# Matmuls of a constant ahead of TensorE's waits in the last batches of a graph-attention kernel's first stage

## The reference

```python
h = maximum(layernorm(x), 0)
Wh = (h @ W).reshape(N, 4, 32)                     # layer 0: attention, four heads
e = leaky_relu(s_src[:, None, :] + s_dst[None, :, :])
att = softmax(where(adj > 0, e, -9e15), axis=1)
x = x + elu(einsum('ijh,jhd->ihd', att, Wh))
h = maximum(layernorm(x), 0)
x = x + where(has_nbr, max over neighbours j of h[j], 0)    # layer 1: maximum
```

## Time and profile before

| | us |
|---|---|
| median of 3 runs | 626.85 (613.61 to 634.16) |
| the profiled execution | 619.35, span 617.6 |
| PE busy / DVE busy / POOL busy | 348.8 / 350.5 / 332.1 |
| ACT busy | 154.7 |
| stage one's part of the span | up to about 381.6 |
| mean granted TensorE clock | 0.715 of full |

### The profile page before, as it was taken

One profiled execution on the slowest core, in us unless ns is written; L12 is line 12 of the kernel. 1 busy time (PEld: TensorE's weight loads), 2 busy tenths in 40 slices (PEclk: granted clock), 3 DMA queues, 4 the chain that ended last, 5 costly groups with the idle time before them and its releaser, 6 DMA issues. The chain is left out here.

```text
span 617.6 us, 8203 instructions
## 1 busy us (share of the span) xinstructions
PE 348.8 (56%) x2410; PEld 258.7 (42%) x2410; DVE 350.5 (57%) x1375; ACT 154.7 (25%) x429; POOL 332.1 (54%) x360
## 2 busy tenths in 40 slices
PE   1847667592939385461707371511755666566764
PEld 1732334361617153251707370301643554455553
DVE  7976767772928284572818656311644554454575
ACT  1731312321314142432413242100111111121122
POOL 7927075254555637274563703774665666666620
PEclk9958588697878879595856696555677667666578
DMA  8938999994979869127120401121121122222211
GB/s 294 418 127 314 399 357 402 364 377 145 369 237 382 296 247 339 50 57 287 41 55 10 136 26 51 52 55 34 47 53 47 48 59 57 55 57 64 61 39 33
DMA packets 28740, 100.97 MB, mean 163 GB/s; under 512 B 6869, under 2 KB 13397, under 8 KB 20501
## 3 DMA queue, kind: packets, MB, share of 16 engines
q1 hardware_dynamic: 16245, 76.33, 31.8%
q0 software_dynamic: 9344, 19.75, 13.1%
q10 hardware_dynamic: 3104, 4.33, 1.9%
HBM read 93.92 MB, written 6.46 MB: 163 GB/s over the span
## 5 line engine op out<-in xcount | busy, mean ns | idle before, releaser
L711 POOL DMA_INDIRECT G<-wh_table,idx x146 | 149.3, 1022 | 112.2 <-DVE idx L1266 70.8
L1481 POOL DMA_INDIRECT G<-h_table,idx x146 | 137.8, 944 | 75.9 <-issue 35.5
L1546 DVE TENSOR_TENSOR_SCAN S<-adjf,S,psf 128x128 f32<-128x128 bf16 x107 | 51.0, 477 | 83.8 <-remote 38.7
L1513 PE MATMUL psf<-identf,S 128*128 128x128 f32 x146 | 58.1, 398 | 71.5 <-issue 53.7
L1522 PE MATMUL psf<-Sb,OL 128*128 128x128 f32 x292 | 85.2, 389 | 19.3 <-issue 12.2
L1493 ACT COPY Sb<-psf 128x128 f32<-128x128 f32 x146 | 37.4, 266 | 194.3 <-PE psf L1513 86.7
L883 PE MATMUL psf<-adjf,packw 128*128 128x512 f16 x256 | 75.1, 437 | 16.2 <-DMA adjf<-in_adj_dram 13.7
L1522 PEld LDWEIGHTS psf<-Sb,OL 128*128 128x128 f32 x292 | 67.3, 285 | 28.7 <-issue 19.8
L1513 PEld LDWEIGHTS psf<-identf,S 128*128 128x128 f32 x146 | 28.4, 195 | 86.5 <-issue 63.5
L1507 PE MATMUL psf<-identf,G 128*128 128x128 f32 x146 | 54.8, 375 | 6.6 <-DMA G<-h_table,idx 5.2
L961 PE MATMUL psf<-Xb,Rm 128*128 128x24 bf16 (+3 forms) x292 | 14.1, 185 | 71.8 <-DVE Rm L1216 71.8
(11 more groups left out here) (165 smaller groups left out, 564.9 us busy)
## 6 DMA issues: line engine op xcount, KB each, us to landing
adjf<-in_adj_dram SPq DMA_DIRECT2D x64, 1024.0 KB
adjf<-keep_table SPq DMA_DIRECT2D x4, 960.0 KB
G<-wh_table,idx POOLq DMA_INDIRECT x146
G<-h_table,idx POOLq DMA_INDIRECT x146
out_dram<-rows_out SPq DMA_DIRECT2D x32, 64.0 KB
wh_table<-OQ ACTq DMA_DIRECT2D x7, 272.0 KB, 8.5
h_table<-h1b ACTq DMA_DIRECT2D x3, 384.0 KB
xsf<-in_x_dram SPq DMA_DIRECT2D x2, 512.0 KB, 9.7
```

The lines of the kernel that those rows point to most:

```text
L711: pool.indirect_dma_start(G[:, plan.at[k] + b, :], None, wh_table, bass.IndirectOffsetOnAxis(ap=idx[:, n:n + 1], axis=0)).then_inc(gathere ...
L1481: pool.indirect_dma_start(G1[:, n % NG, :], None, h1_table, bass.IndirectOffsetOnAxis(ap=idx[:, n:n + 1], axis=0)).then_inc(found[n % NG], 16)
L1513: nc.tensor.transpose(ps[:, BACK[m % 3], 0:P], S[:, m % 5, :], ident[:, :]).then_inc(back_done, 1)
L1546: V.tensor_tensor_scan(S[:, n % 5, :], flags[:, n * P:(n + 1) * P], ps[:, n % 3, 0:P], start, ALU.mult, ALU.max).then_inc(scan_done, 1)
```

## The change

`keep_warm(n)` issues n matmuls with the identity `identb` (128 by 128, bf16) as weights and the first 512 columns of `packw` as the streamed operand into bank 1 of `psf`. Nobody reads the result. It does nothing until `warm` is set: that is at k = 8, in which TensorE first waits until ScalarE has summed and VectorE has taken all words, so that bank 1 is free. It is called at five places of the loop. That gives 8 + 12 + 8 + 8 = 36 matmuls for k = 8 (six units in `select`), 8 + 8 + 8 + 8 = 32 for k = 9 (four units), and 8 + 8 for each of k = 10 and 11: 100 in all. No other engine's program changes. Lines below 935 move down by 8 to 12 in the changed file.

```diff
             packs = 0
+            warm = False
+            filler = packw[:, :, :].rearrange("p k q -> p (k q)")[:, 0:512]
...
+            def keep_warm(n):
+                if warm:
+                    for _ in range(n):
+                        nc.tensor.matmul(ps[:, 1, :], identb[:, :], filler, start=True, stop=True)
...
                 pe.wait_ge(xb_ready, k + 1)
                 for u, unit in enumerate(plan.batches[k]):
+                    keep_warm(2)
                     pe.wait_ge(r_ready, plan.unit0[k] + u + 1)
...
                 if k < NBT:
                     offsets(k)
+                if k and not warm and taken(k - 1, POINTS - 1) == NV:
+                    warm = True
+                    pe.wait_ge(words_summed, T)
+                    pe.wait_ge(words_used, NV)
+                keep_warm(8)
                 max_back(k - 2)
...
                 pack_to(words_free(k, 1))
+                keep_warm(8)
                 if k == NBT:
                     aggregate(k - 2, slice(0, 3))
...
                     aggregate(k - 2)
                     if 0 <= k - 1 < NBT:
+                        keep_warm(8)
                         scores_by_row(k - 1)
```

## The result

| | us |
|---|---|
| before, median of 4 runs | 624.13 (613.61 to 634.16) |
| after, median of 4 runs | 634.33 (633.7 to 638.19) |
| ratio | 1.0285, 95% interval 1.0154 to 1.0417 |
| profiled execution, before / after | 619.35 / 634.76, spans 617.6 / 631.0 |
| first gather of stage two starts at | 382.36 / 396.57 |

The account below looks back on a forecast made before the run. The bound was VectorE's work up to the indices, the run of gathers, then TensorE's late word. 6.6 us through k = 9 plus 0.4 after gave +7.0: 626.4, scaled to the median 634 us, range 617 to 650.

Parts of the forecast that it names:

- The eight fillers ahead of line 947 at k = 8: They fall into TensorE's 4.91 us of idle time before 278.17 and cost nothing.
- the words come at once: Rival: a TensorE busy just before `max_back` gets its word out at once; -15 us, 612 us; chance 0.1.
- `select` at k = 8: Ten uncovered fillers end the selection 4.3 us later; VectorE's line 1228 is put off by 0.8 us.
- The scores of line 985 end at 312.6: At k = 8, fillers in the selection and two groups of eight delay TensorE's scores from 305.6 to 312.6.
- k = 8 costs +0.8 us: Whole cost at k = 8: +0.8 us, or 3.8 if the scores' word waits for the gathers' end.
- words are late for what TensorE sends: Rival: each filler and weight load adds to what TensorE reports while gathers run; +17 us, 644 us; chance 0.2.
- by depth, not by count: Argument that the rows of k = 8 and 9 differ by place in the run of gathers, not number sent.
- the scores' word 3 us late: At k = 9, the word is sent 10.1 us into the gathers; line 1294 starts at 349.6 instead of 341.75.
- the sign that was named for "wrong": TensorE's words heard at once during gathers, or line 1294 at k = 9 within 0.2 us of the scores' end.
- k = 10 and 11: Fillers behind line 1316 at k = 10: net +0.4 us, bounds -0.8 and +3.4.
- the clock's gain of 1.5: Eight fillers ahead of the aggregate leave a high clock for three tiles at 351.81: gain 1.5 us, at most 2.6.
- Stage two: 0: TensorE stands idle for over 10 us before stage two, so nothing is handed over: 0 us.

Follow-up runs that it names:

- e9: Only the 32 fillers ahead of aggregate and scores at k = 8 and 9 kept, in a 624 us job: 630.01 us, 1.0134 against the kernel before.
- b1: The kernel before, unchanged, measured and profiled again: 623.2 us beside 624.0 for the same kernel.
- a1: The changed kernel with all 100 fillers, measured and profiled again: 636.58 us, 1.0263 against the kernel before.
- e1: Only the 16 fillers ahead of line 947's maxima at k = 8 and 9 kept: 520.98 against 520.8 us for the kernel before, 0.999.
- e8: Only the 32 fillers of k = 10 and 11 kept: 522.05 against 521.78 us for the kernel before, 0.9996.
- e3: Only the 32 fillers ahead of aggregate and scores at k = 8 and 9 kept, in a 521 us job: 521.26 us, 1.0014 against the kernel before.
- e5: All fillers of the changed kernel split into four of 128 columns, 400 in all: 525.29 against 521.78 us for the kernel before, 1.0086.

## Why the prediction was right, and where it was not

The time named, 634, was met (634.33), and the sign. That the time was met is luck: +7.0 us or 1.1% was forecast; measured are +10.2 by the medians, 15.4 between the profiled executions and 2.85% (17.8 us) by the ratio. The new runs of the kernel before lowered its median from the 626.85 that I scaled to 624.13, which hid part of the difference. The mechanism held in part: the cost does lie in what TensorE has to tell while gathers run, but the step that was to be nearly free, k = 8, is the dearest.

The lengths of the turns, from one start of line 1316 (1332 in the changed kernel, 1330 in e9) to the next, give the cost step by step; in the two profiles of the kernel before they agree within 0.1 us:

| us | before | b1 | after | a1 | e9 | forecast | after - before | a1 - b1 |
|---|---|---|---|---|---|---|---|---|
| k = 8 to 9 | 35.41 | 35.39 | 42.02 | 41.99 | 39.06 | +0.8 | +6.6 | +6.6 |
| k = 9 to 10 | 21.93 | 21.92 | 24.99 | 28.10 | 28.83 | +5.8 | +3.1 | +6.2 |
| k = 10 to 11 | 15.79 | 15.69 | 17.31 | 16.66 | 15.12 | +0.4 | +1.5 | +1.0 |
| k = 11 to stage two's first gather | 19.18 | 19.17 | 20.36 | 19.17 | 19.36 | 0 | +1.2 | 0.0 |
| time less span | 1.75 | 1.57 | 3.76 | 4.03 | 1.72 | 0 | +2.0 | +2.5 |

- **The eight fillers ahead of line 947 at k = 8** cost nothing, as forecast, and brought nothing: line 1316 came 1.84 us later, but this shift is older than they are. The first filler starts at 274.27; ahead of it, the run of gathers of batch 7 was already 1.8 us late (its one gather of 1.25 us starts at 272.94 instead of 271.14), and in both profiles the word comes 2.7 us after that run's last gather. So the rival "the words come at once" fails too. These are the last gathers before and after:

```profile
286.44 0.94 POOL L711 DMA_INDIRECT G<-wh_table,idx  x1 [0.30 <-issue]
```

```profile
288.23 0.94 POOL L711 DMA_INDIRECT G<-wh_table,idx  x1 [0.30 <-issue]
```

- **The price of a filler** held: 1.89 us for eight at the high clock, 3.58 at the low one (forecast 1.8 and 3.4).
- **`select` at k = 8** held: the transposes start at 298.46 instead of 292.96, 3.7 us beyond the shift (forecast 4.3), and line 1228 0.5 us (forecast 0.8; 1.1 between a1 and b1).
- **"The scores of line 985 end at 312.6" failed**, and with it "k = 8 costs +0.8 us". Two things were not in it. The aggregate's own words became late: its last tile waits 3.00 us for ScalarE's copy of the tile two before, and VectorE gets the last one at 319.48. And TensorE itself stood still within the scores, which end at 329.6. The gathers' end, taken as the bound for words, is a bound for TensorE's work too. Line 1316 at k = 9 came 6.6 us beyond the shift, where 0.8 was the forecast and 3.8 its bound. This speaks for the rival "words are late for what TensorE sends", which had 0.2. Its sum of +17 us is nearer than the forecast's 7 to the 15.4 and the 17.8, but it had put 3.8 at k = 8 and 10 at k = 9, and no profile shows it so. Its argument against, that the rows differ "by depth, not by count", was read from too few words.
- **k = 9, "the scores' word 3 us late"**: in the first profile it came at once: line 1310 starts at 352.44 behind scores that ran from 348.21 to 352.3, 8 us into the run of gathers. This is the sign that was named for "wrong". The maxima's word behind it is 3.4 us late (355.45 to 358.90), and the turn cost 3.1 us instead of 5.8. In a1 the scores' word is 2.3 us late and the turn cost 6.2, as forecast, but not by the forecast's path. The fillers were to put the scores four to six us farther back against their batch's first gather; they start 3.9 us behind it in the first profile and 2.1 in a1, against 1.7 in both profiles of before, since much of the work ahead of them (the selection's later fillers, all transposes and tiles) now ran at the high clock. A word sent 8 us into the run was prompt and one sent 6.3 us into it late, so depth in the run alone does not decide either.
- **k = 10 and 11** came to +1.5 at the last maxima instead of +0.4: the eight fillers ahead of them cost what was said, but the clock's gain of 1.5 did not come. The first tile takes 1.69 us as before, at a granted clock of 0.50 from 363 to 368: the eight fillers from 355.30 ran at 1.00 and had 6.09 us of idle time behind them. After the last maxima another 1.2 us went, as two tiles from 382.29 on, of 0.9 us before, took 1.6 each; between b1 and a1 nothing went there.
- **Stage two: 0** held, 235.2 against 234.4 us. The 2.0 to 2.5 us outside the span were in no term of the sum.
- A slip in the reading of the earlier trace rows: 21.6 us over 17 steps are 1.27 us per gather and not 1.25, which changes nothing.
- On the rule from the Trainium skill, page "TensorE: Matmul & The Clock Gate", Part 2 (matmuls keep program order), the trace agrees: the last line 955 starts 1.72 us behind the start of its eight fillers (375.72 behind 374.00) with its operands there.
- The Trainium skill, the same page, "Why this matters for your kernels", advises to leave TensorE no long idle gaps between bursts, so that its clock stays up. In e1 and e8 the clock did rise, and the time stayed (0.999 and 0.9996): for this kernel the advice brings nothing. That the work at the low clock was mostly hidden behind VectorE is read from the waits and not tested by itself.

What stays open: what it is in two of the five jobs that makes TensorE's words late, whether a run without indirect gathers would free them there, and whether number or time of the fillers counts. The halts follow the fillers in three profiles of two jobs (after, a1, e9) and are missing in both profiles of the kernel before; that they need the gathers is only read from where they begin and end. So the backlog is the reading that fits best, and is not shown.

One rival is untested and would explain much: that it is the recording of the execution that backs up. All executions here were recorded, and the records themselves differ between the jobs. For the kernel before and for e3 the profile's list of transfers says:

```profile
G<-h_table,idx POOLq DMA_INDIRECT x146
```

```profile
G<-h_table,idx POOLq DMA_INDIRECT x146, 2.5
```

The median time to landing, 2.5 us, stands only in the second, since in the first most landings have no record: 16 updates for each of the 146 gathers make 2336, of which its trace holds 443 and that of e3 2331. The traces of the five profiles with late words hold 4428 to 4582 semaphore updates, those of the nine with prompt words 9290 to 9319, for nearly the same program. Whether late words lose the records, or the recording makes the words late, no run tells, as there is none without it.

## What to carry to other kernels

Work in an engine's idle time may still not be free, if something else of that engine is short: here every instruction seems to add to what TensorE has to report, and where words were late, two groups of eight ahead of waited-for work were enough (e9) to turn a late word into an engine that stood still. Before trading anything for a higher clock, find work at the low clock that something waits for: in this stretch it was at most 5 us by the prediction's count, and the fillers did not win it. And when a wait's end is put down to no instruction, compare it with the end of the releasing engine's work, and time the kernel again elsewhere: the 100 us between 521 and 624 dwarf the change. Compare time and span as well: some 2.4 us of this change's cost stood in no timeline.

## What the runs showed of the hardware

- The same kernel took 521 to 522 us in three jobs and 624 in two. Where it took 624, TensorE's semaphore signals to VectorE came up to 11.2 us late during runs of indirect gathers issued by GpSimd, some of them 2.65 us and some at once; in e3, of a job with 521, the waits they ended were of 0.2 us.
- In the former, with fillers ahead of them, TensorE's fp32 passes were mostly 1.4 to 2.8 us apart (0.11 normally, 4.13 / 36), with nothing to wait for, up to 2.5 us after the last gather.
- The profiles of the former hold 4428 to 4582 semaphore updates, those of the latter 9290 to 9319.
- 100 fillers more made an execution 2.4 us longer outside its span (3.8 to 4.4 us against 1.5 to 1.9), 400 narrow ones did not (e5).
- After eight matmuls of 512 columns at a granted clock of 1.00 and 6.09 us of idle time behind them, the next tiles ran at 0.50.
